# The last two feed-forward chunks of a layer stack, interleaved behind a shorter drain

## The chip, the cores and the metric

The kernel runs on one core of one Trainium2 chip. The metric is device time in microseconds (us) of one execution, start to end. Engines are called TensorE (PE, with PEld for its weight loads), VectorE (DVE), ScalarE (ACT), GpSimd (POOL) and SyncE (SP, which here only issues DMAs).

## The reference

The input is `x` of shape (2, 1024, 128), 2048 tokens of 128 features. Four stages follow: full causal attention (a), a stack of six layers (b), a gated linear scan (c), and the stack again. A stack takes the layer norm of its input, runs six layers on it and adds the result to its input. One layer is local attention and a feed-forward part, each with a residual:

```python
def attn_layer(x, Wqkv, qs, ksc, Wo): ...      # token shift first; 16 heads of 64, window 32
def ffn_layer(x, g, bln, W1, b1, W2, b2):      # on the token-shifted x
    mu = x.mean(-1, keepdims=True)
    var = ((x - mu) ** 2).mean(-1, keepdims=True)
    xn = (x - mu) / jnp.sqrt(var + 1e-05) * g + bln
    hg = xn @ W1 + b1
    a, gate = jnp.split(hg, 2, -1)             # 341 columns each
    return a * jax.nn.gelu(gate, approximate=False) @ W2 + b2
```

The token shift gives half of the features (64) the value of the token before.

## The kernel before

Activations lie transposed: 128 features on the partitions, 2048 tokens along the free dimension, in four chunks of 512 (`NC`, `CH`, `cs(k)`). `xT` is the residual of the whole network, `y` the running value inside a stack, `xs` the token-shifted copy of `y` that the projections read. All matrix products are fp32; one product of 128x512 is two MATMUL instructions in the trace. PSUM has eight banks of 128x512, `bank[0]` to `bank[7]`.

`stack(rep, ...)` is called twice. In it each engine has one program and semaphores order them; nothing is planned at run time. A layer is 32 slots (`PER`): the pairs of heads by chunks, 16 slots (`HALF`) for chunks 0 and 1 and 16 for chunks 2 and 3. `pipelined` writes out the slots: once for the first layer, a loop for the next five, and then `LAG` slots that drain what is still in flight. In slot `j`, `unit(k)` is the work that began `k` slots ago: projections at 0, scores at 2, the value product and output projection at 4, and VectorE's addition into `y` (L1112) at 5. So attention alone needs five draining slots.

The feed-forward part lags by `FLAG` = 19 slots and takes six slots per chunk (`ffn`, `FSTEPS`), one link of its chain in each: 0 mean (L982) and centring (L1115); 1 square (L1038), variance (L985), and ScalarE's Ln and Exp (L1017, L1035); 2 to 4 gain (L1144), bias (L1059), and one of `FT` = 3 pairs of W1 products each, `a` (L972) into bank 7 and `g` (L987) into bank 1, copied out with biases by VectorE (L1119) and ScalarE (L1021); 5 the GELU table load (L1069), the GELU (L1071) and GpSimd's product `hid*gel` (L828). Then W2's products (L976) and VectorE's addition (L1122). In the loop these links lie between attention work. After the last layer, two chunks remain when attention has ended: `LAG` = `HALF` + 1 = 17 draining slots, of which the slots from 3 on hold the twelve steps of chunk 2 and then chunk 3. There is one set of buffers (`fin`, `gel`, `hid`, `fsq`, `frs`), and each step waits for the step before it. SyncE shifts `y` into `xs` by two DMAs per chunk (L746). At the very end VectorE waits for all and adds `y` to `xT` in four instructions (L1164). The block ends there; stage c's first block follows the first stack, and the block with the output transposes (L206), ScalarE's copies (L214) and output DMAs (L222) follows the second.

Of the kernel before, what the change touches and what calls it, by code (L numbers as in the profile page):

```python
# [8 lines left out]
ALU = mybir.AluOpType  # L9
ACT = mybir.ActivationFunctionType  # L10
AX = mybir.AxisListType

P = 128
# [3 lines left out]
NC = N // CH  # L17
# [6 lines left out]
DEPTH, HEADS, DH, WIN = 6, 16, 64, 32  # L24
# [7 lines left out]
FT = -(-FI // P)  # L32
# [18 lines left out]
ONE = 1  # L51


def pipelined(eng, per, count, lag, slot, peel_last=False):


    def run(it, first=False, end=False):
        for j in range(lag if end else per):
            def unit(k, j=j):
                back, jj = divmod(j - k, per)  # L60
                if (first and back < 0) or (end and back >= 0):
                    return None
# [564 lines left out]
def stack(rep, ln_call, S, nc, w, c, bank, wide, xT, y, ident, identb, jmean, ln_eps, ss_eps, ss_back,  # L627
# [3 lines left out]
    with ExitStack() as st:  # L631
        def sb(name, shape, dt=F32):
            return st.enter_context(nc.sbuf_tensor(f"b{rep}_{name}", shape, dt))

        PAD = BLK
        xs = sb("xs", [P, N])
# [17 lines left out]
        prc = sb("prc", [P, 4, 2, CH])  # L654
# [11 lines left out]
        hid = sb("hid", [P, FT, CH])  # L666
        fin, gel = cen[:, 0, :], cen[:, 1:1 + FT, :]
        fsq, frs = sqr[:, 2, :], sqr[:, 3, :]

        L0 = DEPTH * rep  # L670
        FIRST = 1
        PER = 2 * 2 * PAIRS
        HALF = PER // 2
        FLAG = HALF + 3
        FSTEPS = 6
        LAG = HALF + 1
        ZERO = 8

        def um(u):
            return PER * (L0 + u[0]) + u[1], u[1] % 4  # L680
# [4 lines left out]
        def pair(u):  # L685
            return u[1] % HALF // 2

        def chunk(u):
            return 2 * (u[1] // HALF) + u[1] % 2

        def ffn(u):
            if u is None or u[1] % HALF >= 2 * FSTEPS:
                return None, None, None
            which, step = divmod(u[1] % HALF, FSTEPS)
            k = 2 * (u[1] // HALF) + which
            return step, k, NC * (L0 + u[0]) + k

        def ffn_out(u):
            if u is None or u[1] % HALF not in (FSTEPS, 2 * FSTEPS):
                return None, None  # L700
            k = 2 * (u[1] // HALF) + u[1] % HALF // FSTEPS - 1
            return k, NC * (L0 + u[0]) + k

        def closes(u):
            return pair(u) == PAIRS - 1
# [6 lines left out]
        with nc.Block() as block:  # L712
            @block.sync
            def _(sp):
# [23 lines left out]

                def slot(j, unit, sp=sp):
                    a, b, e = unit(0), unit(1), unit(5)  # L740
                    if e and closes(e):
                        C = NC * (L0 + e[0]) + chunk(e)
                        sp.wait_ge(S["y_add"], ONE + um(e)[0] + 1)
                        sp.wait_ge(S["fin_done"], ONE + 32 * C)
                        for to, frm in shifted(chunk(e)):
                            sp.dma_start(to, frm).then_inc(S["fin_done"], 16)  # L746
                    if b:
                        U, r = um(b)
                        sp.wait_ge(S["va_cp"], ONE + U + 1)
                        sp.wait_ge(S["vs_ld"], ONE + 32 * U)  # L750
                        sp.dma_start(vs[0:BLK, 4 * r:4 * r + 4, :], va[BLK:P, 4 * r:4 * r + 4, :]).then_inc(S["vs_ld"], 16)
                        sp.dma_start(vs[BLK:P, 4 * r:4 * r + 4, :], va[0:BLK, 4 * r + 1:4 * r + 5, :]).then_inc(S["vs_ld"], 16)
                        if b[1] > HALF and b[1] % 2 and not (isinstance(b[0], int) and b[0] == DEPTH - 1):
                            sp.wait_ge(S["va_mm"], ONE + U + 1)
                            sp.wait_ge(S["wqkv_ld"], ONE + 16 * (PAIRS * (L0 + b[0] + 1) + pair(b)))
                            load_qkv(b[0] + 1, pair(b))
                    if e:
                        U, r = um(e)
                        if e[1] > HALF and e[1] % 2 and not (isinstance(e[0], int) and e[0] == DEPTH - 1):
                            sp.wait_ge(S["wo_mm"], ONE + U + 1)  # L760
                            sp.wait_ge(S["wo_ld"], ONE + 16 * (PAIRS * (L0 + e[0] + 1) + pair(e)))
                            load_wo(e[0] + 1, pair(e))
                    if a and HALF <= j < HALF + 3:
                        li = a[0]
                        f = "L0_ffn_"
                        ffw = []
                        for i in range(2):
                            ffw.append((w1[:, i, 0:FI], w[f + "W1"][li, :, i * FI:(i + 1) * FI]))
                        for dst, nm in ((lng[:, 0:1], "ln_g"), (lng[:, 1:2], "ln_b"), (b2[:, 0:1], "b2")):
                            ffw.append((dst, w[f + nm][li, :].rearrange("(p a) -> p a", a=1)))  # L770
                        for h in range(2):
                            for i in range(FT):
                                n = P if i < FT - 1 else FR
                                ffw.append((b1[0:n, h, i:i + 1], w[f + "b1"][li, h * FI + i * P:h * FI + i * P + n]
                                            .rearrange("(p a) -> p a", a=1)))
                        ffw.append((w2[:, 0:FT - 1, :], w[f + "W2"][li, 0:(FT - 1) * P, :].rearrange("(i p) d -> p i d", p=P)))
                        ffw.append((w2[0:FR, FT - 1, :], w[f + "W2"][li, (FT - 1) * P:FI, :]))
                        if j == HALF and not (isinstance(li, int) and li == 0):
                            sp.wait_ge(S["y_done"], ONE + NC * (L0 + li))
                        for dst, src in ffw[5 * (j - HALF):5 * (j - HALF) + 5]:  # L780
                            sp.dma_start(dst, src).then_inc(S["ffw_ld"], 16)
                    if a:
                        U, r = um(a)
                        sp.wait_ge(S["pk_done"], ONE + U + 1)
                        if b:
# [12 lines left out]
                pipelined(sp, PER, DEPTH, LAG, slot, peel_last=True)  # L798

            @block.gpsimd  # L800
            def _(pool):
# [9 lines left out]
                def slot(j, unit, pool=pool):  # L811
# [13 lines left out]
                    if step == 5:  # L825
                        pool.wait_ge(S["f_acp"], ONE + FT * C + FT)
                        pool.wait_ge(S["f_gelu"], ONE + C + 1)
                        pool.tensor_tensor(hid[:, :, :], hid[:, :, :], gel, ALU.mult).then_inc(S["f_hid"], 1)  # L828
                pipelined(pool, PER, DEPTH, LAG, slot)

            @block.tensor
            def _(pe):
# [155 lines left out]

                pipelined(pe, PER, DEPTH, LAG, slot)

            @block.scalar
            def _(act):
                ln_act(act, ln_call)
# [2 lines left out]
                def slot(j, unit, act=act):  # L996
# [75 lines left out]
                pipelined(act, PER, DEPTH, LAG, slot)  # L1072

            @block.vector
            def _(dve):
# [22 lines left out]
                def slot(j, unit, dve=dve):  # L1098
# [845 lines left out]
```

## Time and profile before

| | us |
|---|---|
| median of 3 runs | 4513.82 (4508.88 to 4517.1) |
| the profiled execution | 4512.5 |
| its span, first to last instruction | 4510.8 |
| TensorE / VectorE / ScalarE / GpSimd busy | 4195.9 / 3451.3 / 3074.1 / 1811.6 |

The span leaves out 1.7 us of the profiled execution's time, which lie around it. Busy time is a mean over stages of different kinds and does not tell what bounds one of them. The mean granted TensorE clock is 0.959 of full speed.

### The profile page before, as it was taken

How to read it: one execution, taken by the hardware profiler on the slowest of the kernel's cores; microseconds unless marked ns; L12 is line 12 of the kernel's file. 1: busy time of each engine (PE TensorE's matmuls, PEld its weight loads, DVE VectorE, ACT ScalarE, POOL GpSimd, SP SyncE). 2: the span in 40 equal slices, each digit the busy share in tenths (PEclk: the TensorE clock that was granted, in tenths of full speed). 3: DMA queues.
4: the chain of work that ended last, by engine and by line, in shares of the span. 5: the costliest groups of instructions: out<-in, count | busy, mean ns of one | idle time of the engine just before them, and what ended most of it. 6: DMA issues, size and time to landing. Idle time of an engine off the chain costs nothing. (4 is left out here: it accounts for less than half of the span.)

```text
span 4510.8 us, 115928 instructions
## 1 busy us (share of the span) xinstructions
PE 4195.9 (93%) x44625; PEld 2511.7 (56%) x44625; DVE 3451.3 (77%) x4977; ACT 3074.1 (68%) x7028; POOL 1811.6 (40%) x1075
## 2 busy tenths in 40 slices
PE   7998999999999999999867589999999999999996
PEld 3443565655656655556436446555566556565663
DVE  5774888888888888888625478888888888888883
ACT  3555777777777777777652267777777777777774
POOL 3112444444444444444314434444444444444442
PEclk8997999999999999999976699999999999999998
DMA  2113444444443444444200044434444444444331
GB/s 42 30 21 83 99 100 99 103 103 93 105 104 88 106 99 103 99 92 98 61 10 3 3 122 108 101 85 110 101 96 101 97 102 101 94 104 105 89 92 36
DMA packets 239318, 382.06 MB, mean 85 GB/s; under 512 B 65636, under 2 KB 128736, under 8 KB 238472
## 3 DMA queue, kind: packets, MB, share of 16 engines
q1 hardware_dynamic: 238344, 373.28, 35.9%
q8 instruction: 386, 6.32, 0.6%
q10 hardware_dynamic: 384, 0.79, 0.1%
q14 instruction: 204, 1.67, 0.1%
HBM read 39.22 MB, written 1.05 MB: 9 GB/s over the span
## 5 line engine op out<-in xcount | busy, mean ns | idle before, releaser
L816 POOL TENSOR_TENSOR b_prob<-b_prob,b_rinv 128x768 f32<-128x768 f32 x384 | 565.1, 1472 | 1894.2 <-DVE b_rinv L1152 1894.2
L822 POOL TENSOR_TENSOR b_prc<-b_prc,b_sws 128x1024 f32<-128x1024 f32 x384 | 907.5, 2363 | 62.5 <-DMA b_sws<-b_prs 62.4
L1065 ACT ACTIVATE b_prob<-ps,b_nmx 128x96 f32<-128x96 f32 x3072 | 751.1, 363 | 0.0
L860 PEld LDWEIGHTS ps<-ident,b_prob 128*128 128x128 f32 x3072 | 378.1, 141 | 419.5 <-issue 297.4
L1093 DVE SCALAR_TENSOR_TENSOR b_prc<-ps,b_qks,b_rot 128x512 f32<-128x512 f32 x768 | 570.5, 743 | 12.8 <-ACT b_sq L1028 12.1
L1095 DVE SCALAR_TENSOR_TENSOR b_prs<-ps,b_qks,b_rot 128x512 f32<-128x512 f32 x768 | 569.3, 741 | 0.0
L1133 DVE TENSOR_TENSOR b_prc<-b_prc,ps 128x512 f32<-128x512 f32 x384 | 263.5, 686 | 387.2 <-PE ps L916 321.3
L1048 ACT ACTIVATE b_oT<-ps 128x512 f32<-128x512 f32 x384 | 227.2, 592 | 359.5 <-PE ps L874 359.5
L860 PE MATMUL ps<-ident,b_prob 128*128 128x128 f32 x3072 | 464.4, 274 | 4.4 <-ACT b_pT L1003 4.4
L1106 DVE SCALAR_TENSOR_TENSOR b_rsp<-b_rhi,b_minus_hi,b_rn 128x512 fp32r<-128x512 f32 x192 | 376.0, 1959 | 115.5 <-ACT b_rn L1014 115.5
L951 PE MATMUL ps<-b_wqkv,b_xs 128*128 128x128 f32 x3072 | 446.5, 289 | 1.4 <-DVE b_prs L1095 1.2
L1003 ACT ACTIVATE b_pT<-ps 128x512 f32<-128x512 f32 x724 | 436.3, 603 | 14.6 <-PE ps L860 11.1
L874 PE MATMUL ps<-b_pT,b_vs 128*64 128x64 f32 x6144 | 436.7, 234 | 0.3
L905 PE MATMUL ps<-b_xs,b_wqkv 128*128 128x512 f32 x768 | 405.6, 610 | 22.1 <-issue 14.6
L965 PE MATMUL ps<-b_oT,b_wo 128*128 128x512 f32 x768 | 412.3, 619 | 5.6 <-ACT b_oT L1048 5.6
L874 PE MATMUL ps<-b_pT,b_va 128*64 128x64 f32 x6144 | 399.6, 222 | 0.0
L921 PE MATMUL ps<-b_xs,b_wqkv 128*128 128x512 f32 x768 | 396.4, 597 | 0.5
L951 PEld LDWEIGHTS ps<-b_wqkv,b_xs 128*128 128x128 f32 x3072 | 373.3, 192 | 33.1 <-issue 7.3
L1157 DVE TENSOR_REDUCE b_nmx<-ps 128x8 f32<-128x768 f32 x384 | 353.3, 920 | 48.6 <-PE ps L940 48.1
L874 PEld LDWEIGHTS ps<-b_pT,b_vs 128*64 128x64 f32 x6144 | 307.7, 136 | 110.9 <-issue 64.5
L1149 DVE TENSOR_REDUCE b_ssm<-b_prob 128x8 f32<-128x768 f32 x384 | 361.5, 942 | 0.0
L1041 ACT ACTIVATE b_sq<-ps 128x512 f32<-128x512 f32 x384 | 229.4, 597 | 176.5 <-PE ps L921 174.9
(252 smaller groups left out, 7275.2 us busy)
## 6 DMA issues: line engine op xcount, KB each, us to landing
b_sws<-b_prs SPq DMA_DIRECT2D x1536, 128.0 KB, 2.3
b_vs<-b_va SPq DMA_DIRECT2D x768, 128.0 KB, 2.4
b_wqkv<-in_L_ffn_Wqkv SPq DMA_DIRECT2D x96, 192.0 KB, 2.8
b_xs<-y SPq DMA_DIRECT2D x132, 128.0 KB, 2.4
b_wo<-in_L_ffn_Wo SPq DMA_DIRECT2D x96, 64.0 KB, 2.2
b_xs<-y SPq DMA_DIRECT2D x44, 127.8 KB, 2.4
b_rot<-in_rot SPq DMA_DIRECT2D x2, 2048.0 KB, 7.8
b_w<-in_L_ffn_W SPq DMA_DIRECT2D x24, 170.5 KB
```

The source lines that it names most:

```text
L816: pool.tensor_tensor(prob[:, r, :, P - KEYS:P], prob[:, r, :, P - KEYS:P], rinv[:, r % 2, :].rearrange("p (b a) -> p b a", a=1).broadcast_ ...
L822: pool.tensor_tensor(prc[:, r, :, :], prc[:, r, :, :], sws[:, r % 2, :, :], ALU.add)\
L860: t = pe.transpose(bank[6][:, i * P:(i + 1) * P], prob[:, kd, 4 * e + 2 * h + m, :], ident[:, :])
L874: t = pe.matmul(bank[7][es, n * BLK:(n + 1) * BLK], v[:, es], pT[:, h, 2 * e + m, o * BLK:(o + 1) * BLK], start=(n == 0), stop=(n == NB - ...
L905: pe.matmul(bank[0][:, :], W[:, 0, :], X, start=True, stop=True).then_inc(S["q_mm"], 1)
L921: pe.matmul(bank[1][:, :], W[:, 1, :], X, start=True, stop=True).then_inc(S["k_mm"], 1)
L951: m = pe.matmul(bank[0][:, t * P:(t + 1) * P], xs[:, at:at + P], W[:, 2, :], start=(t == 0), stop=(t == 3), skip_group_check=True)
L965: pe.matmul(bank[3][:, :], wo[:, pair(d), :], oT[:, kd % 2, :], start=True, stop=True).then_inc(S["wo_mm"], 1)
L1003: act.activation(pT[:, h, :, :], bank[6].rearrange("p (i q) -> p i q", i=4), ACT.Copy)\
L1065: g = act.activation(prob[:, kb, i, P - KEYS:P], wide[0][:, e * CH + m * KEYS:e * CH + (m + 1) * KEYS], ACT.Exp, bias=nmx[:, kb % 2, i:i + 1])
L1093: dve.scalar_tensor_tensor(out=prc[:, r, i, :], in0=bank[i][:, :], scalar=scale, in1=rot[:, 2 * i, t], op0=ALU.mult, op1=ALU.mult)
L1095: dve.scalar_tensor_tensor(out=prs[:, r % 2, i, :], in0=bank[i][:, :], scalar=scale, in1=rot[:, 2 * i + 1, t], op0=ALU.mult, op1=ALU.mult) ...
```

## The change

The drain becomes five slots. The feed-forward parts of chunks 2 and 3 of the last layer leave the slots (`ending`) and are written out behind them, step by step for both chunks in turn. The second chunk has buffers of its own in tiles that attention no longer uses (`sqr`, `sq`, and `prc` as `more`), and the products have a bank each as far as eight reach. The shift of the two chunks goes from SyncE's DMAs to ScalarE copies, the product `hid*gel` from GpSimd to VectorE, and `y` is no longer summed first for these chunks: `add_x` adds it to `xT` early, and the last instruction adds W2's result to `xT` directly. Below, after the helpers, the new code of TensorE, then ScalarE's order, then VectorE's.

```diff
-        LAG = HALF + 1
+        LAG = 5
...
+        def ending(u):
+            return isinstance(u[0], int) and u[0] == DEPTH - 1 and u[1] >= HALF
...
-            if u is None or u[1] % HALF >= 2 * FSTEPS:
+            if u is None or ending(u) or u[1] % HALF >= 2 * FSTEPS:
...
+        end_fin, end_fsq, end_frs = (fin, sqr[:, 0, :]), (fsq, sqr[:, 1, :]), (frs, sq[:, 0, :])
+        end_gel, end_hid = (gel, sq[:, 1:1 + FT, :]), (hid[:, :, :], more[:, 0:FT, :])
+        end_mean, end_var, end_out = (0, 1), (2, 4), (0, 2)
+        end_g, end_a = ((5, 6, 0), (1, 5, 6)), ((7, 3, 2), (4, 7, 3))
...
-                    if e and closes(e):
+                    if e and closes(e) and not ending(e):
...
+                for n in range(2):
...
+                    pe.wait_ge(S["fin_done"], ONE + 32 * (CEND + n + 1))
+                    pe.matmul(bank[end_mean[n]], jmean[:, :], xs[:, cs(2 + n)], start=True, stop=True).then_inc(S["f_mean"], 1)
...
+                for n in range(2):
+                    pe.wait_ge(S["f_sq"], ONE + CEND + n + 1)
+                    pe.matmul(bank[end_var[n]], jmean[:, :], end_fsq[n], start=True, stop=True).then_inc(S["f_var"], 1)
...
+                for n in range(2):
+                    pe.wait_ge(S["f_in"], ONE + CEND + n + 1)
+                    for i in range(FT):
...
+                        elif n == 1:
+                            pe.wait_ge(S["f_gcp"], ONE + FT * CEND + i)
+                            pe.wait_ge(S["f_acp"], ONE + FT * CEND + i)
+                        pe.matmul(bank[end_g[n][i]], w1[:, 1, i * P:(i + 1) * P], end_fin[n], start=True, stop=True)\
+                            .then_inc(S["f_g"], 1)
+                        pe.matmul(bank[end_a[n][i]], w1[:, 0, i * P:(i + 1) * P], end_fin[n], start=True, stop=True)\
+                            .then_inc(S["f_a"], 1)
...
+                for n in range(2):
+                    pe.wait_ge(S["f_hid"], ONE + CEND + n + 1)
+                    for i in range(FT):
+                        m = pe.matmul(bank[end_out[n]], w2[:, i, :], end_hid[n][:, i, :], start=(i == 0), stop=(i == FT - 1))
+                    m.then_inc(S["f_out"], 1)
...
+                last_shift(0)
+                last_square(0)
+                last_shift(1)
+                last_rstd(0)
+                last_square(1)
+                last_in(0)
+                last_rstd(1)
+                last_in(1)
+                act.preload_act_table_set("gelu_and_others")
+                last_gate(0)
+                last_gelu(0)
+                last_gate(1)
+                last_gelu(1)
+                act.preload_act_table_set("natural_log_exp_and_others")
...
-                dve.wait_ge(S["y_done"], ONE + NC * (L0 + DEPTH))
-                for k in range(NC):
...
+                def last_product(n, dve=dve):
+                    dve.wait_ge(S["f_acp"], ONE + FT * (CEND + n) + FT)
+                    dve.wait_ge(S["f_gelu"], ONE + CEND + n + 1)
+                    dve.tensor_tensor(end_hid[n], end_hid[n], end_gel[n], ALU.mult).then_inc(S["f_hid"], 1)
...
+                add_x(0)
+                last_cen(0)
+                last_cen(1)
+                add_x(1)
+                last_norm(0)
+                last_norm(1)
+                for i in range(FT):
+                    last_hidden(0, i)
+                add_x(2)
+                add_x(3)
+                last_hidden(1, 0)
+                last_product(0)
+                last_hidden(1, 1)
+                last_hidden(1, 2)
+                last_out(0)
+                last_product(1)
+                last_out(1)
```

The helpers are what their names say: ScalarE's `last_shift` is two copies (`shifted(2 + n)`), of 64 partitions each, `last_square`, `last_rstd` (Ln, Exp), `last_in` (bias), `last_gate` (three copies with bias) and `last_gelu` (one instruction of 128x1536) do what L1038, L1017 with L1035, L1059, L1021 and L1071 did; `last_cen`, `last_norm` and `last_hidden` do what L1115, L1144 and L1119 did; `last_out` adds bank, bias `b2` and `xT` into `xT`.

## Rows read from the trace of the kernel before

**Rows 1.** Page, TensorE's granted clock in 40 slices of the span, tenths of full

```profile
PEclk8997999999999999999976699999999999999998
```

**Rows 2.** Windows from last y addition to block's end: us, busy by engine, clock, DMA

```profile
2233.75:2291.36 57.61, 27.51 (x43) 9.70 (x42) 11.29 (x16) 17.56 (x20) 6.83 (x2) 0.82 0.02 5
...
4443.71:4503.21 59.50, 29.41 (x43) 10.18 (x42) 11.29 (x17) 17.55 (x20) 6.83 (x2) 0.76 0.02 5
```

**Rows 3.** Timeline, SyncE's queue: start us, duration us, instruction

```profile
4438.77 6.07 SPq L746 DMA_DIRECT2D b_xs<-y  x4
```

**Rows 4.** Timeline, end of the second stack: start us, duration us, instruction, idle before it

```profile
4441.21 0.60 ACT L1048 ACTIVATE b_oT<-ps 128x512 f32<-128x512 f32 x1 [0.79 <-PE ps L874]
...
4443.02 0.69 DVE L1112 TENSOR_TENSOR y<-ps,y 128x512 f32<-128x512 f32 x1 [4.28 <-PE ps L965]
...
4444.60 0.63 ACT L1038 ACTIVATE sqr<-cen 128x512 f32<-128x512 f32 x1 [2.79 <-DVE cen L1115]
...
4445.37 1.10 PE L985 MATMUL ps<-sqr,jmean 128*128 128x512 f32 x2 [1.53 <-ACT sqr L1038]
4446.51 0.69 ACT L1017 ACTIVATE sqr<-ps,ln_eps 128x512 f32<-128x512 f32 x1 [1.28 <-PE ps L985]
...
4449.54 2.04 PE L972 MATMUL ps<-cen,b_w 128*128 128x512 f32 x2 [3.07 <-ACT cen L1059]
```

**Rows 5.** Groups by line in 4443.7 to 4503.3: busy us, mean ns, idle us before

```profile
L976 PE MATMUL ps<-b_hid,b_w 128*128 128x512 f32 x12 | 9.4, 948 | 14.5 <-POOL b_hid L828 14.5
...
L828 POOL TENSOR_TENSOR b_hid<-b_hid,cen 128x1536 f32<-128x1536 f32 x2 | 6.8, 3417 | 51.8 <-ACT cen L1071 51.8
L1119 DVE TENSOR_SCALAR b_hid<-ps,b_b 128x512 f32<-128x512 f32 x6 | 4.5, 750 | 17.1 <-PE ps L972 17.1
L1021 ACT ACTIVATE cen<-ps,b_b 128x512 f32<-128x512 f32 x6 | 4.1, 688 | 17.6 <-PE ps L987 17.6
...
L1071 ACT ACTIVATE cen<-cen 128x1536 f32<-128x1536 f32 x2 | 3.0, 1482 | 0.0
L1069 ACT ACT_TABLE_LOAD x2 | 2.6, 1283 | 0.0
...
L1164 DVE TENSOR_TENSOR xT<-xT,y 128x512 f32<-128x512 f32 x4 | 2.5, 686 | 0.0
...
L1144 DVE SCALAR_TENSOR_TENSOR cen<-cen,b_lng,sqr 128x512 f32<-128x512 f32 x2 | 1.5, 752 | 6.0 <-ACT sqr L1035 6.0
L1122 DVE SCALAR_TENSOR_TENSOR y<-ps,b_b,y 128x512 f32<-128x512 f32 x2 | 1.5, 748 | 12.0 <-PE ps L976 12.0
L1059 ACT ACTIVATE cen<-cen,b_lng 128x512 f32<-128x512 f32 x2 | 1.4, 721 | 1.6 <-DVE cen L1144 1.6
L1115 DVE TENSOR_TENSOR cen<-b_xs,ps 128x512 f32<-128x512 f32 x2 | 1.4, 687 | 13.1 <-PE ps L982 13.1
L1017 ACT ACTIVATE sqr<-ps,ln_eps 128x512 f32<-128x512 f32 x2 | 1.4, 687 | 2.6 <-PE ps L985 2.6
```

**Rows 6.** Timeline, the six W2 instructions of an earlier chunk, inside the loop

```profile
4416.46 2.74 PE L976 MATMUL ps<-b_hid,b_w 128*128 128x512 f32 x6
```

**Rows 7.** Windows of TensorE alone: us, busy, clock, DMA share, GB/s

```profile
2239.50:2242.70 3.20, 3.12 (x4) 0.50 0.00 0
4448.00:4458.00 10.00, 7.53 (x8) 0.50 0.00 0
4503.50:4507.20 3.70, 3.65 (x16) 0.50 0.26 72
```

**Rows 8.** Groups by line, VectorE, whole span: a product of 128x1536

```profile
L1755 DVE TENSOR_TENSOR c_bl<-ps,c_lmask 128x1536 f32<-128x1536 f32 x8 | 14.0, 1747 | 0.0
```

**Rows 9.** Timeline, the last block: the output transposes and the copies

```profile
4503.54 3.65 PE L206 MATMUL ps<-ident,xT 128*128 128x128 f32 x16 [3.65 <-PEq L712]
4504.66 0.60 ACT L214 ACTIVATE otok<-ps 128x512 f32<-128x512 f32 x1 [11.86 <-PE ps L206]
...
4507.22 0.60 ACT L214 ACTIVATE otok<-ps 128x512 f32<-128x512 f32 x1 [0.26 <-PE ps L206]
```

More of the change, by code:

```diff
@@ L698, in ffn_out @@
         def ffn_out(u):
-            if u is None or u[1] % HALF not in (FSTEPS, 2 * FSTEPS):
+            if u is None or ending(u) or u[1] % HALF not in (FSTEPS, 2 * FSTEPS):
                 return None, None
@@ L702, in ffn_out @@
             return k, NC * (L0 + u[0]) + k
+        UALL, CEND = PER * (L0 + DEPTH), NC * (L0 + DEPTH - 1) + 2
+        more = prc[:, :, :, :].rearrange("p a b c -> p (a b) c")
+        end_fin, end_fsq, end_frs = (fin, sqr[:, 0, :]), (fsq, sqr[:, 1, :]), (frs, sq[:, 0, :])
+        end_gel, end_hid = (gel, sq[:, 1:1 + FT, :]), (hid[:, :, :], more[:, 0:FT, :])
+        end_mean, end_var, end_out = (0, 1), (2, 4), (0, 2)
+        end_g, end_a = ((5, 6, 0), (1, 5, 6)), ((7, 3, 2), (4, 7, 3))
         def closes(u):
@@ L989, in _ @@
                 pipelined(pe, PER, DEPTH, LAG, slot)
+                pe.wait_ge(S["va_cp"], ONE + UALL)
+                for n in range(2):
+                    if n == 1:
+                        pe.wait_ge(S["pk_done"], ONE + UALL)
+                        pe.wait_ge(S["f_gcp"], ONE + FT * CEND)
+                    pe.wait_ge(S["fin_done"], ONE + 32 * (CEND + n + 1))
+                    pe.matmul(bank[end_mean[n]], jmean[:, :], xs[:, cs(2 + n)], start=True, stop=True).then_inc(S["f_mean"], 1)
@@ new lines, in _ @@
+                pe.wait_ge(S["qn_done"], ONE + UALL)
+                pe.wait_ge(S["exp_done"], ONE + UALL)
+                for n in range(2):
+                    pe.wait_ge(S["f_sq"], ONE + CEND + n + 1)
+                    pe.matmul(bank[end_var[n]], jmean[:, :], end_fsq[n], start=True, stop=True).then_inc(S["f_var"], 1)
+                pe.wait_ge(S["pt_cp"], ONE + 2 * UALL)
+                pe.wait_ge(S["o_cp"], ONE + UALL)
+                pe.wait_ge(S["y_done"], ONE + CEND)
+                pe.wait_ge(S["y_add"], ONE + UALL)
@@ new lines, in _ @@
+                for n in range(2):
+                    pe.wait_ge(S["f_in"], ONE + CEND + n + 1)
+                    for i in range(FT):
+                        if n == 0 and i == 2:
+                            pe.wait_ge(S["f_cen"], ONE + CEND + 1)
+                            pe.wait_ge(S["f_lnv"], ONE + CEND + 1)
+                        elif n == 1 and i == 0:
+                            pe.wait_ge(S["f_cen"], ONE + CEND + 2)
+                            pe.wait_ge(S["f_lnv"], ONE + CEND + 2)
+                        elif n == 1:
[5 more added lines that the diff above has]
+                            .then_inc(S["f_a"], 1)
@@ L991, in _ @@
+                pe.wait_ge(S["f_gcp"], ONE + FT * CEND + FT)
+                pe.wait_ge(S["f_acp"], ONE + FT * CEND + FT)
+                for n in range(2):
[3 more added lines that the diff above has]
+                    m.then_inc(S["f_out"], 1)
             @block.scalar
@@ L1072, in _, with last_shift, last_square, last_rstd @@
                 pipelined(act, PER, DEPTH, LAG, slot)
+                def last_shift(n, act=act):
+                    act.wait_ge(S["y_add"], ONE + UALL - 1 + n)
+                    act.wait_ge(S["va_mm"], ONE + UALL)
+                    for to, frm in shifted(2 + n):
+                        act.activation(to, frm, ACT.Copy).then_inc(S["fin_done"], 16)
+                def last_square(n, act=act):
+                    act.wait_ge(S["f_cen"], ONE + CEND + n + 1)
+                    act.activation(end_fsq[n], end_fin[n], ACT.Square).then_inc(S["f_sq"], 1)
+                def last_rstd(n, act=act):
+                    act.wait_ge(S["f_var"], ONE + CEND + n + 1)
+                    act.activation(end_frs[n], bank[end_var[n]], ACT.Ln, bias=ln_eps[:, 0:1]).then_inc(S["f_lnv"], 1)
+                    act.wait_ge(S["f_lnv"], ONE + CEND + n + 1)
+                    act.activation(end_frs[n], end_frs[n], ACT.Exp, scale=-0.5).then_inc(S["f_rstd"], 1)
+                def last_in(n, act=act):
+                    act.wait_ge(S["f_norm"], ONE + CEND + n + 1)
+                    act.activation(end_fin[n], end_fin[n], ACT.Identity, bias=lng[:, 1:2]).then_inc(S["f_in"], 1)
+                def last_gate(n, act=act):
+                    for i in range(FT):
+                        act.wait_ge(S["f_g"], ONE + FT * (CEND + n) + i + 1)
+                        act.activation(end_gel[n][:, i, :], bank[end_g[n][i]], ACT.Identity, bias=b1[:, 1, i:i + 1])\
+                            .then_inc(S["f_gcp"], 1)
+                def last_gelu(n, act=act):
+                    act.wait_ge(S["f_gcp"], ONE + FT * (CEND + n) + FT)
+                    act.activation(end_gel[n], end_gel[n], ACT.Gelu).then_inc(S["f_gelu"], 1)
+                last_shift(0)
[12 more added lines that the diff above has]
+                act.preload_act_table_set("natural_log_exp_and_others")
             @block.vector
@@ L1161, in _, with add_x @@
                 pipelined(dve, PER, DEPTH, LAG, slot)
-                dve.wait_ge(S["y_done"], ONE + NC * (L0 + DEPTH))
-                for k in range(NC):
-                    dve.tensor_tensor(xT[:, cs(k)], xT[:, cs(k)], y[:, cs(k)], ALU.add).then_inc(S["x_done"], 1)
+                def add_x(k, dve=dve):
+                    if k < 2:
+                        dve.wait_ge(S["y_done"], ONE + CEND - 1 + k)
+                    else:
+                        dve.wait_ge(S["y_add"], ONE + UALL - 3 + k)
+                    dve.tensor_tensor(xT[:, cs(k)], xT[:, cs(k)], y[:, cs(k)], ALU.add).then_inc(S["x_done"], 1)
@@ new lines, in last_cen, with last_norm @@
+                def last_cen(n, dve=dve):
+                    dve.wait_ge(S["f_mean"], ONE + CEND + n + 1)
+                    dve.tensor_tensor(end_fin[n], xs[:, cs(2 + n)], bank[end_mean[n]], ALU.subtract).then_inc(S["f_cen"], 1)
+                def last_norm(n, dve=dve):
+                    dve.wait_ge(S["f_rstd"], ONE + CEND + n + 1)
+                    dve.scalar_tensor_tensor(out=end_fin[n], in0=end_fin[n], scalar=lng[:, 0:1], in1=end_frs[n],
+                                             op0=ALU.mult, op1=ALU.mult).then_inc(S["f_norm"], 1)
@@ new lines, in last_hidden @@
+                def last_hidden(n, i, dve=dve):
+                    dve.wait_ge(S["f_a"], ONE + FT * (CEND + n) + i + 1)
+                    dve.tensor_scalar(end_hid[n][:, i, :], bank[end_a[n][i]], b1[:, 0, i:i + 1], None, ALU.add).then_inc(S["f_acp"], 1)
+                def last_product(n, dve=dve):
+                    dve.wait_ge(S["f_acp"], ONE + FT * (CEND + n) + FT)
+                    dve.wait_ge(S["f_gelu"], ONE + CEND + n + 1)
+                    dve.tensor_tensor(end_hid[n], end_hid[n], end_gel[n], ALU.mult).then_inc(S["f_hid"], 1)
@@ new lines, in last_out @@
+                def last_out(n, dve=dve):
+                    dve.wait_ge(S["f_out"], ONE + CEND + n + 1)
+                    dve.wait_ge(S["x_done"], ONE + NC * rep + 3 + n)
+                    x = xT[:, cs(2 + n)]
+                    dve.scalar_tensor_tensor(out=x, in0=bank[end_out[n]], scalar=b2[:, 0:1], in1=x, op0=ALU.add, op1=ALU.add)\
+                        .then_inc(S["y_done"], 1)
+                add_x(0)
+                last_cen(0)
+                last_cen(1)
+                add_x(1)
@@ L1167, in stage_c @@
+                last_norm(0)
+                last_norm(1)
+                for i in range(FT):
+                    last_hidden(0, i)
[8 more added lines that the diff above has]
+                last_out(1)
 def stage_c(nc, w, c, sem, ps, bank, xT, y, ident, jmean, ln_eps, cen, sqr, rstd, ln_pe, ln_act, ln_dve, norm_done, cs, ln_call):
```

## The prediction

> **What bounds the kernel now.** I read the page first. TensorE's granted clock is full in all slices of the span but a few: at the start, at the middle (the first stack's end and stage c) and at the very end [rows 1]. The loops of the stacks are TensorE's; the change leaves every slot of them as it is. What it touches comes once per stack, so I cut two windows with one rule: from the end of the last addition into `y` (L1112, the last work of attention) to the end of the block. They last 57.61 us in the first stack and 59.50 us in the second, TensorE is busy for 27.5 and 29.4 of them, VectorE for 11.3, ScalarE for 17.6, and nothing is moved by DMA to speak of [rows 2]. So no engine bounds them: a chain of dependent steps does. The table by line says whose turns these are: GpSimd waits 51.8 us for two products, the W2 products wait 14.5 us for GpSimd, ScalarE's three copies per chunk 17.6 us for TensorE, VectorE's 17.1 us [rows 5]. The next blocks start only when all engines are through, so each microsecond off these windows is one off the kernel.
>
> **The change part by part.** Let 0 be the end of the last L1112, 4443.71 in the second stack (4443.02 + 0.69) [rows 4]. The new tail can be laid out on that scale; what is before 0 stays.
>
> Durations, by row: ScalarE from SBUF 0.63 [rows 4], from PSUM 0.69, with the bias of L1059 0.72, GELU of 1536 columns 1.48, table load 1.28; VectorE 0.69 for centring, 0.75 for L1144, L1119 and L1122, 0.69 for an `xT` addition (0.63 from one to the next in a row of four) [rows 5]. One product is two MATMULs; three of them in a row took 2.74 at full clock inside the loop [rows 6], which is 0.86 each and 0.17 until the last result is out; at half clock 1.71 each. A result passes to ScalarE or VectorE in 0.04 (L985 ends at 4446.47, L1017 starts at 4446.51) [rows 4]; to TensorE in 0.14 (L1038 ends at 4445.23, L985 starts at 4445.37) [rows 4].
>
> Layer norms, at full clock. ScalarE is free from its last `b_oT` copy at 4441.81 [rows 4], which is -1.9. SyncE's four DMAs, 6.07 us with their wait [rows 3], go; chunk 2's had landed before TensorE was free, so here ScalarE's copies (two of 64 partitions each, a form that no row shows; I price each at the 0.63 of 128 partitions, and between half of that and twice that the tail moves by -0.6 to +1.3 for each chunk) put the mean at -0.4, where TensorE is nearly free anyway. Result at 0.64, VectorE after `add_x(0)` centres until 1.37, the square is done at 2.04. Now the order written for ScalarE tells: chunk 3's shift stands behind this square, 2.07 to 3.36, though its data were there at 0. TensorE in turn has chunk 3's mean ahead of chunk 2's variance: 3.50, then the variance's result at 5.39. Ln and Exp to 6.79, gain to 7.58, the bias behind square(1) to 8.34. Chunk 3's variance is at TensorE 7.59 to 8.45, so the W1 products start at 8.48. In the chain before, this stretch took 4449.54 - 4443.71 = 5.8 for one chunk and again, behind the W2 products, for the other.
>
> W1 products: twelve in a row, 12 x 0.86 = 10.3, to 18.8. Beside them ScalarE does Ln, Exp and bias of chunk 3 (to 11.57), the table load (12.88), three copies (15.04) and the GELU (16.55); VectorE copies chunk 2's three `a` results, adds `y` to `xT` twice, and multiplies `hid*gel` until 18.34. This product is new on VectorE: GpSimd's took 3.42 [rows 5]; VectorE's only fp32 product of 128x1536 in the trace took 1.75, one input in PSUM [rows 8]. I take 1.75, the same size on the same engine; bounds are ScalarE's 1.48 for as many columns and GpSimd's 3.42, which would add 1.7 at each of two places. Hand-over of banks does not stop the twelve: the second chunk's later pairs wait for copies that end at 13.6 and 14.3, before TensorE comes to them at 15.4 and 17.1. That is the gain of separate banks: before, every pair waited for the copy of the pair before.
>
> Out: W2 products of chunk 2 from 18.8 with the result at 21.55, VectorE's addition to 22.34. Here again an order costs: chunk 3's product stands behind that addition on VectorE, 22.34 to 24.09, though its GELU was done at 20.35. W2 products 24.23 to 26.98, addition to 27.77. The four final additions (2.5 from first to last) are inside.
>
> So at full clock the new tail is 27.8 us, against 57.6 and 59.5.
>
> **TensorE's clock.** Before, both first W1 stretches ran at half clock: 3.2 us of it shown in the first stack, 10 us in the second [rows 7], after a layer norm in which TensorE stood idle 3.07 us [rows 4]. The new layer norms hold gaps too: 2.9 us between the two means, 2.2 before the second variance. I expect the clock to fall in them and to come back in the dense W1 stretch, as in the first stack. Price: chunk 3's mean and chunk 2's variance 0.86 each, chunk 3's variance and the start of the W1 stretch together 1.7: 3.4, so 31.2 us per tail. If the clock stays full: 27.8. If it is half all along, the second stack's case at its worst: 22 products on TensorE's path (4 means and variances, 12 of W1, 6 of W2), 0.86 each, make 18.9 more, 46.7. The nearest rows are the two stacks before; the denser W1 stretch (twelve products without a wait, where there were two at a time) decides for the lower part. The gap ahead of the last W2 products is 2.7 us, shorter than the 3.07 above, and follows a dense stretch; I count them full.
>
> The clock page of the Trainium skill (TensorE: Matmul & The Clock Gate, Part 1) says that the clock is halved after an idle spell of TensorE and restored by a busy one. The trace agrees on the whole, but the fall before L972 came after a layer norm with products in it [rows 4, 7], so gaps with little work between them are enough here. By that rule of the Trainium skill alone the new layer norms, never idle for long, would keep the clock: that is the first rival below.
>
> The Trainium skill also budgets about 2.7 us for a switch of ScalarE's table (ScalarE: Activation LUTs, Rules for kernel authors). The rows have 1.28 [rows 5]. By that figure of the Trainium skill the first copies would end 1.4 later and so would chunk 2's product, which TensorE waits for: 1.4 per tail more at most. The row decides.
>
> **Next blocks.** The output transposes start after 3.6 us of idle TensorE and ran at half clock, 3.65 us; the fourth copy starts 3.68 behind the first transpose [rows 7, 9]. After the new tail TensorE is idle for about 1.1 us. At full clock the first copy can start 0.5 earlier, and then copies of 0.60 follow each other without waiting, 1.86 from the first to the fourth where it was 2.56: 1.2 us earlier in all. Stage c's first layer norm opens the same way; I put 1.0 there (0 to 2). Together 2.2, 0 if the clock is half.
>
> **Sum.** Second stack 59.5 - 31.2 = 28.3, first 57.6 - 31.2 = 26.4, next blocks 2.2: 56.9 less. On the profiled execution's own 4512.5 us that is 4455.6; on the median of the runs, 1.3 above it, 4456.9, which I round to 4457.
>
> **The rivals.** First, the clock stays full in both tails: for it speaks that no gap is longer than 2.9, against it the fall before. Time: 31.7 + 29.8, and 3 in the next blocks: 64.5 less, 4449. Chance 0.17.
>
> Second, the clock stays half through both tails: the second stack before shows 10 us in one piece while TensorE was busy for 7.5 of them [rows 7]. 12.8 + 10.9 = 23.7 less, 4490. Against it: the W1 stretch is now busy without pause. Chance 0.04.
>
> Third, the interleaving is worth less than it looks: queues in order (VectorE and ScalarE serve both chunks) leave the second chunk waiting in more places than I found, as a wait for a bank that comes on top. If both tails end at 39 instead of 31: 20.5 + 18.6, and 2 in the next blocks, 41 less, 4473. For it speaks that three such places are already in my layout; against it, that they are counted. Chance 0.11.
>
> Fourth, slower than before. The tail itself cannot do it: even at half clock it is shorter. It would have to be the loops, whose code is the same but lies in a program of another length; if instructions came later there, each of some 384 slots would pay. It decides from 57/384 = 0.15 us per slot; at 0.2 us the time would be 4457 + 77 = 4534. Nothing in the rows shows such a stall, and the full clock in the loops [rows 1] speaks against starved engines. Chance 0.02.
>
> My forecast has 0.66. A measurement of this kernel tells 0.2% (9 us) from no change. The forecast and the first three rivals are all faster by more, 0.98 together, of which I move 0.01 to no change for what I have not foreseen; slower keeps 0.02. The range takes the first rival and 3 us for the spread of runs below, 4446, and reaches to near the third above, 4470.
>
> **What would show it.** Windows of 28 to 34 us from the last L1112 to the block's end in both stacks. Twelve W1 products with no gap between them; ScalarE's shift of chunk 3 starting about 2 us after its `y` was ready; the `hid*gel` product on VectorE at 1.75; the clock below full in the layer norms and full at the W2 products; transposes in about 2 us. The loops' slots as long as before. The prediction is wrong if the W1 stretch is broken by waits, if the partial ScalarE copies cost much more than 0.63, if the clock falls again between the two W2 stretches, or if any time moves outside these windows.

## The result, and the profile after

The changed kernel takes 4448.52 us (median of 4 runs, 4442.27 to 4466.87), the kernel before 4513.18 (4 runs). The ratio is 0.986, with a 95% interval of 0.9839 to 0.988: faster, by 64.7 us of medians. The profiled execution took 4450.76, 61.7 less than the one before; its span is 4449.0.

I cut the span at events that both kernels have: the end of the last addition into `y` (L1112, now L1207) in each stack, the end of the last VectorE instruction of the tail, the end of stage c's last addition. Us by stage:

| | first part with stack 1 | tail 1 | stage c | stack 2 | tail 2 | output |
|---|---|---|---|---|---|---|
| before | 2233.75 | 57.61 | 302.31 | 1850.04 | 59.50 | 7.59 |
| after | 2236.03 | 32.03 | 294.24 | 1849.99 | 29.59 | 7.12 |

The windows of the changed kernel (us, then busy time with instructions in brackets for PE, PEld, DVE, ACT, POOL, then clock, DMA share, GB/s), against [rows 2]:

```profile
2236.03:2268.06 32.03, 24.07 (x44) 9.44 (x42) 14.37 (x18) 15.81 (x20) 0.00 (x0) 0.84 0.00 0
2268.06:2562.30 294.24, 185.66 (x5333) 149.27 (x5333) 140.29 (x260) 110.41 (x177) 115.01 (x168) 0.69 0.02 6
4412.29:4441.88 29.59, 21.63 (x44) 8.42 (x42) 14.37 (x19) 15.70 (x20) 0.00 (x0) 0.88 0.00 0
4441.88:4449.00 7.12, 1.94 (x16) 1.73 (x16) 0.00 (x1) 2.07 (x4) 0.00 (x0) 0.87 0.56 150
```

A tail is the stretch in the second column, from the last addition into `y` to the block's end. TensorE is now busy for 24.1 and 21.6 us of the two tails, three quarters of them; before it was less than half. The clock is 0.84 and 0.88, not full. Stage c, which was not touched, lost 8 us too; I come back to it.

The timeline of the second tail (start us, duration us, instruction, idle before it), against [rows 4]:

```profile
4410.28 1.27 ACT L1128 ACTIVATE b_xs<-y 64x512 f32<-64x512 f32 x2
...
4411.60 0.69 DVE L1207 TENSOR_TENSOR y<-ps,y 128x512 f32<-128x512 f32 x1 [4.28 <-PE ps L975]
...
4413.55 0.63 ACT L1132 ACTIVATE sqr<-cen 128x512 f32<-128x512 f32 x1 [2.00 <-DVE cen L1267]
4414.08 1.26 ACT L1128 ACTIVATE b_xs<-y 64x512 f32<-64x512 f32 x2
...
4415.49 1.16 PE L1007 MATMUL ps<-b_xs,jmean 128*128 128x512 f32 x2 [2.70 <-ACT b_xs L1128]
...
4416.44 1.92 PE L1012 MATMUL ps<-sqr,jmean 128*128 128x512 f32 x2
...
4422.18 1.54 PE L1029 MATMUL ps<-cen,b_w 128*128 128x512 f32 x2
...
4427.85 1.02 PE L1029 MATMUL ps<-sqr,b_w 128*128 128x512 f32 x2
...
4430.59 1.75 DVE L1281 TENSOR_TENSOR b_hid<-b_hid,cen 128x1536 f32<-128x1536 f32 x1
...
4433.00 2.74 PE L1038 MATMUL ps<-b_hid,b_w 128*128 128x512 f32 x6
...
4433.06 1.48 ACT L1152 ACTIVATE b_sq<-b_sq 128x1536 f32<-128x1536 f32 x1
...
4435.78 0.75 DVE L1287 SCALAR_TENSOR_TENSOR xT<-ps,b_b,xT 128x512 f32<-128x512 f32 x1 [1.82 <-PE ps L1038]
4436.45 1.75 DVE L1281 TENSOR_TENSOR b_prc<-b_prc,b_sq 128x1536 f32<-128x1536 f32 x1
...
4438.25 2.84 PE L1038 MATMUL ps<-b_prc,b_w 128*128 128x512 f32 x6 [2.51 <-DVE b_prc L1281]
...
4441.13 0.75 DVE L1287 SCALAR_TENSOR_TENSOR xT<-ps,b_b,xT 128x512 f32<-128x512 f32 x1 [2.94 <-PE ps L1038]
...
4442.21 1.94 PE L206 MATMUL ps<-ident,xT 128*128 128x128 f32 x16 [1.12 <-PEq L722]
```

0 is 4412.29 here. Chunk 3's shift (the two ScalarE copies at 4414.08) starts 1.79 after its `y` was ready, behind chunk 2's square. Its mean and the variance behind it fill 4415.49 to 4418.36. The W1 products start at 9.89 and run without a gap from chunk 2 into chunk 3 to the W2 products at 20.71. Chunk 3's GELU ends at 4434.54 and its product starts 1.91 later, behind chunk 2's last addition. The transposes follow at 1.94 us for all sixteen, where they took 3.65 [rows 9].

TensorE's clock in it (us, busy time, clock, DMA share, GB/s), against [rows 7]:

```profile
4415.50:4422.10 6.60, 4.64 (x6) 0.57 0.00 0
4423.60:4441.80 18.20, 14.98 (x35) 1.00 0.00 0
2262.90:2267.20 4.30, 4.29 (x6) 0.64 0.00 0
```

It was half for most of the stretch from the second mean into the first W1 product, full from there to the end in tail 2; in tail 1 it was half again at the start of the last W2 products, after a pause of 2.51 us, and they took 4.36 us instead of 2.84:

```profile
2262.91 4.36 PE L1038 MATMUL ps<-b_prc,b_w 128*128 128x512 f32 x6 [2.51 <-DVE b_prc L1281]
```

### The profile page after: what moved, and what is told of

Read it like the earlier page. It is cut to its first block and busy times, and to the rows that moved or that the text cites. A ratio compares the mean times of both kernels' runs of the same rounds, so it can differ in the third digit from the quotient of the medians.

```text
span 4449.0 us, 115926 instructions
## 1 busy us (share of the span) xinstructions
PE 4171.8 (94%) x44625; PEld 2499.4 (56%) x44625; DVE 3462.9 (78%) x4981; ACT 3073.0 (69%) x7032; POOL 1796.9 (40%) x1071
## 5 line engine op out<-in xcount | busy, mean ns | idle before, releaser
L1115 ACT ACTIVATE b_prob<-ps,b_nmx 128x96 f32<-128x96 f32 x3072 | 751.1, 363 | 0.0
L915 PE MATMUL ps<-b_xs,b_wqkv 128*128 128x512 f32 x768 | 405.6, 610 | 23.8 <-issue 15.4
L931 PE MATMUL ps<-b_xs,b_wqkv 128*128 128x512 f32 x768 | 395.9, 597 | 0.5
```

The source lines that it names most:

```text
L915: pe.matmul(bank[0][:, :], W[:, 0, :], X, start=True, stop=True).then_inc(S["q_mm"], 1)
L931: pe.matmul(bank[1][:, :], W[:, 1, :], X, start=True, stop=True).then_inc(S["k_mm"], 1)
L1115: g = act.activation(prob[:, kb, i, P - KEYS:P], wide[0][:, e * CH + m * KEYS:e * CH + (m + 1) * KEYS], ACT.Exp, bias=nmx[:, kb % 2, i:i + 1])
```

## The experiments

Each starts from the changed kernel, unless it says otherwise. Tails are in the order first, second. The swaps, the filled kernel and the changed kernel beside them were executed four times each, both together six times; the others once. The same kernel's stages differ from run to run, by the clock above all: the changed tails measured 29.6 to 32.0 us, so a single tail tells nothing below 2 us.

**One chunk after the other.** The banks, buffers, VectorE's product, the early additions and ScalarE's shift stay; only the order of each engine is serial:

```diff
-                last_shift(0)
-                last_square(0)
-                last_shift(1)
...
+                last_shift(0)
+                for n in range(2):
+                    last_square(n)
+                    last_rstd(n)
+                    last_in(n)
+                    act.preload_act_table_set("gelu_and_others")
+                    last_gate(n)
+                    last_gelu(n)
+                    act.preload_act_table_set("natural_log_exp_and_others")
+                    if n == 0:
+                        last_shift(1)
```

and likewise on TensorE and VectorE.

> The two chunks one after the other, all else as in the changed kernel (banks, VectorE's product, early additions to xT, ScalarE's shift). My theory: most of the gain is the interleaving. Each chunk's chain alone is about 19 us at full clock (6 for the layer norm, 5.3 for the six W1 products, 4 until the product hid*gel is made, 3 for W2), and half clock after each pause adds 2 to 3, so the tails are 41 to 46 us, 12 to 15 longer than interleaved. Rival: the gain is in the cheaper links (GpSimd's product to VectorE, additions moved, a bank for each product): then the tails stay below 36 us. No change to the kernel: near 58.

Measured: tails 44.89 and 44.96 us, 4482.21 us in all. Its first tail in the view by windows:

```profile
2229.31:2274.20 44.89, 27.97 (x44) 10.08 (x42) 14.65 (x18) 18.81 (x22) 0.00 (x0) 0.81 0.00 0
```

So the gain per tail has two halves: 12.7 and 14.5 us come from the cheaper links, 13 to 15 from the interleaving. "Most of it is the interleaving" was too much; "below 36" was wrong. Of the first half, by rows of before, 3.3 are two products at 1.75 instead of 3.42 [rows 5, 8] and 2.5 the four additions [rows 5]. Two more terms stand in the traces. ScalarE's table load, which stood between the last copy and the GELU before, is hidden under the W1 products here: 1.28 for each chunk, 2.6 in all. The first line is before, the second the serial order:

```profile
4461.36 1.28 ACT L1069 ACT_TABLE_LOAD   x1
...
4434.32 1.28 ACT L1148 ACT_TABLE_LOAD   x1
```

And from the first W1 product to the end of the last copy the second tail took 11.8 and 9.6 us for the two chunks before, 6.9 and 7.0 in the serial order: 7.6 less, for a bank to each product and for the clock, which no run separates. The four make 16.0 of the 14.5 measured in this tail; the serial order gives 1.5 back elsewhere.

**The product back on GpSimd.**

```diff
-                last_product(0)
...
-                last_product(1)
...
+                for n in range(2):                       # after GpSimd's slots
+                    pool.wait_ge(S["f_acp"], ONE + FT * (CEND + n) + FT)
+                    pool.wait_ge(S["f_gelu"], ONE + CEND + n + 1)
+                    pool.tensor_tensor(end_hid[n], end_hid[n], end_gel[n], ALU.mult).then_inc(S["f_hid"], 1)
```

> The two products hid*gel of the tail back on GpSimd. GpSimd takes 3.42 us, VectorE 1.75. My theory: GpSimd begins when the GELU is done and is not behind VectorE's other work, so the first W2 stretch starts about 0.6 us later and the second at the same time or 0.1 earlier: tails within 1 us of the changed kernel's 32.0 and 29.6. Rival: the faster product is a full term of the gain, 1.7 at each of two places, tails 3.3 us longer.

Tails 29.51 and 30.78, 4456.86 us in all: no loss against the four tails of the changed kernel (29.6 to 32.0). In this order the faster product buys nothing, since TensorE is busy with W1 during the first, and the second stood in VectorE's queue: in the second tail, from chunk 3's GELU to its W2 products it is 3.71 us with VectorE's 1.91 of waiting and 1.75 of work, and 3.62 with GpSimd's 3.42. So the prediction's bound for this term, 1.7 more at each of two places with GpSimd's time, was too wide: its layout has room for the second (GELU done at 20.35, the product on VectorE at 24.09), and the first held TensorE for 0.3 us only. Whether the product counts in the serial order or after the swaps below, no run shows.

**The shift back on SyncE's DMAs**, ScalarE's `last_shift` left out:

```diff
+                for n in range(2):                       # after SyncE's slots
+                    sp.wait_ge(S["y_add"], ONE + UALL - 1 + n)
+                    for to, frm in shifted(2 + n):
+                        sp.dma_start(to, frm).then_inc(S["fin_done"], 16)
```

> The shift of the last two chunks back to SyncE's DMAs, ScalarE's four copies left out. Chunk 3's copies end 3.05 us after the last y addition in the changed kernel; two DMA issues and some 2.4 us until they land end at about 2.9 to 3.1. My theory: tails equal within 0.6 us. Rival: ScalarE's copies are a gain of their own against the DMAs: tails 1 to 2 us longer.

Tails 30.66 and 30.70, 4450.84 us: equal within the spread. Chunk 3's mean, which waits for the shift, started 3.04 us after the last `y` addition with the DMAs and 3.20 with the copies. A copy of 64 partitions took ScalarE 0.62; moving the shift there bought nothing.

**Two swaps of order.**

```diff
-                last_square(0)
                 last_shift(1)
+                last_square(0)
...
-                last_out(0)
                 last_product(1)
+                last_out(0)
```

> Two swaps of order, nothing else: ScalarE shifts chunk 3 before it squares chunk 2, and VectorE makes chunk 3's product hid*gel before it adds chunk 2's W2 result. My theory, by the changed kernel's trace: chunk 3's shift can end at 1.3 instead of 3.05 after the last y addition, and its mean and chunk 2's variance behind it come 1.75 earlier; chunk 3's product can start at 22.3 instead of 24.2, so the last W2 stretch starts 1.8 earlier. Tails 3.6 us shorter, near 26 and 28. Rival: these waits are not what ends last and the clock eats what they give (the clock falls anyway): under 1 us.

4438.45 us (4435.72 to 4439.05, 4 runs); the changed kernel, timed beside it on the same chip, 4448.95 (4446.12 to 4452.07, 4 runs). Ratio to before 0.9825 (0.9806 to 0.9845). Tails 24.00 and 25.70, 6.7 and 3.9 less than the changed kernel's second profile. The timeline of its second tail, where 0 is 4404.49:

```profile
4404.58 1.28 ACT L1128 ACTIVATE b_xs<-y 64x512 f32<-64x512 f32 x2 [0.83 <-issue]
...
4423.10 2.74 PE L1038 MATMUL ps<-b_hid,b_w 128*128 128x512 f32 x6
...
4424.75 1.76 DVE L1281 TENSOR_TENSOR b_prc<-b_prc,b_sq 128x1536 f32<-128x1536 f32 x1 [0.70 <-ACT b_sq L1152]
...
4426.56 0.30 PEld L1038 LDWEIGHTS ps<-b_prc,b_w 128*128 128x128 f32 x2 [1.55 <-DVE b_prc L1281]
```

The shift starts at 0.1; chunk 3's product waits for its GELU alone and is under way while W2 of chunk 2 runs, so TensorE stands 0.72 us between the two W2 stretches instead of 2.51. Both tails gained more than the 3.6 expected. In the first the clock was 1.00 throughout, and 24.0 is 3.5 under the 27.5 that the changed order takes at full clock (next experiment): the other 3.3 there are the clock. In the second, with the same pauses, the first W1 products ran at half clock and the mean was 0.93, so closing these pauses does not keep the clock every time. This is the best version that I ran.

**Filled pauses.** Eight products whose results nobody reads, put into TensorE's three pauses:

```diff
+                def idle(m):
+                    for _ in range(m):
+                        pe.matmul(bank[6], jmean[:, :], xs[:, cs(0)], start=True, stop=True)
```

three after the first mean, two before the second variance, three before the last W2 stretch (after a wait for all `f_gcp`).

> The changed kernel, with products whose results nobody reads in TensorE's pauses of the tail (three between the two means, two ahead of the second variance, three ahead of the last W2 stretch), to keep the clock up. My theory: half clock costs the changed tails 1.9 and 4.2 us over the layout at full clock; filled, both tails are 27 to 28.5 us, the granted clock 1.00 in them. Rival: the clock falls all the same, or the filling delays what waits behind it: 29.5 to 32 as before or more.

Tails 27.47 and 27.48 us, clock 1.00:

```profile
4423.58:4451.06 27.48, 26.32 (x60) 1.00 0.00 1
```

That is the layout at full clock, 27.8, within 0.3 (W1 from 8.2, W2 from 18.6, the last W2 from 23.8, where the layout has 8.5, 18.8 and 24.2), and so the clock's share of the changed kernel's tails is 2.1 to 4.6 us. But the kernel got slower: 4464.97 us (4459.91 to 4470.96, 4 runs) against 4448.95. All of it is in stack 2, 1872.84 us. Its layers 2 to 5 took 311.5, 310.8, 312.0 and 308.4 where they have 305 to 307 in the changed kernel; stack 1 is unchanged. The waits of TensorE's matmuls over the loop of stack 2 (us in total, times, longest), filled kernel:

```profile
PE ps L915 <- issue: 15.1, 4, 4.1
```

and changed kernel:

```profile
PE ps L915 <- issue: 3.5, 4, 1.2
```

This wait comes once per turn, at the first instruction of the loop's body. TensorE's timeline at one turn of the filled kernel:

```profile
3776.89 1.45 PE L986 MATMUL ps<-b_hid,b_w 128*128 128x512 f32 x3
3782.45 2.07 PE L915 MATMUL ps<-b_xs,b_wqkv 128*128 128x512 f32 x2 [4.11 <-issue]
...
3786.03 1.91 PE L931 MATMUL ps<-b_xs,b_wqkv 128*128 128x512 f32 x2
```

It stood 4.1 us with all inputs there, and the clock had fallen when it came back: the products L915 and L931 take 2.07 and 1.91 instead of 1.1 and 1.0.

**Both together.**

> Both: the two swaps and the filled pauses. If the two act on different terms, they add up: tails of 24 to 25 us at full clock, some 11 us less than the changed kernel over the two tails, 4439 where it has 4450. If they pay for the same pause, 26 to 27.

4466.15 us (4454.7 to 4471.65, 6 runs); tails 26.91 and 26.92. They do not add up: with the pauses closed by the swaps, the filling stands in the way of what it waited for. In the second tail chunk 3's product was ready at 4453.52, but its W2 products started at 4455.26, behind the filling. The tails are 1.2 and 2.9 us longer than with the swaps alone. Stack 2 is slow again, 1873.16.

**What makes stack 2's loop slow.** Filling in one tail only (`if rep == 0`, `if rep == 1`), then in the first tail with products of 8 columns instead of 512, then only three of these. They were executed once each, on another chip, where the kernel before took 4526.14 us, so their totals are not compared with the others; the stages and turns are:

> The changed kernel with the eight unread products in the first stack's tail alone. In the kernel filled in both, the layers 2 to 5 of the second stack took 311 us instead of 306: TensorE stood 3.8 us at each turn of its loop, where it is 0.9. My theory: what is put ahead of that loop in TensorE's program does it, so with the filling in the first tail alone the second stack is again near 1874 us, its turns 12 to 13 us from y addition to y addition instead of 8. Rival: the filling of the second tail, or the full clock at the end, is what matters: 1850 to 1858.

> The changed kernel with the eight unread products in the second stack's tail alone. Theory: nothing is put ahead of either loop, both stacks as in the changed kernel (1850 to 1858 us for the second), the second tail 27.5, the first 30.5 to 32. Rival: second stack near 1874.

> As the filling in the first tail alone, at the same places and in the same number, but each product 8 columns wide instead of 512: the same instructions, next to no time. If the number of instructions ahead of the loop decides, the second stack is near 1874 us. If what the products do to TensorE (clock, heat, time) decides, it is 1850 to 1858. [...]

> As before, but three short products instead of eight. If any instructions ahead of the loop do it: near 1874 us. If it is a matter of where the loop comes to lie: anything between 1850 and 1874, and the turns of the loop show which.

| | stack 2, us | a turn, y addition to y addition, us | total |
|---|---|---|---|
| changed kernel | 1849.99, 1850.45 | 7.7 to 8.5 | 4450.76, 4446.12 |
| eight in the first tail | 1868.34 | 10.7 to 12.7 | 4470.48 |
| eight in the second tail | 1853.40 | 7.7 to 8.4 | 4450.19 |
| eight short ones in the first | 1874.42 | 10.3 to 14.4 | 4468.97 |
| three short ones in the first | 1858.75 | 8.9 to 9.5 | 4456.03 |

The waits in the kernel with the eight short ones, and below them those in the kernel with three:

```profile
PE ps L915 <- issue: 16.2, 4, 4.5
...
PE ps L926 <- issue: 4.6, 4, 1.4
PE ps L915 <- issue: 3.2, 4, 1.0
```

So neither the work of the filling does it nor the clock (in the first tail 1.00 with the eight long ones, 0.88 with the eight short ones), but instructions ahead of the loop in TensorE's program. Three cost 1.2 us a turn, eight 2 to 6. With three the wait at L915 is what it was, and the new one stands at L926, a little further on in the body: the number of instructions ahead decides also where in the loop TensorE waits. That it is the fetch of the loop's code from another place I only infer; no view shows it. The turns carry this reading, not the totals of stack 2: in the nine runs with nothing put ahead of its loop, stack 2 took 1850.0 to 1856.1.

**The two kernels once more.**

> The kernel before once more, for the spread of the stages that the change does not touch. In the two profiles stage c took 302.3 us before and 294.2 after. If that is the clock's spread from run to run, this run's stage c can lie anywhere between 290 and 306 and the tails repeat near 58 and 59 (within 3 us, by the clock). If the change makes stage c shorter, this run shows 302 within 1 us.

> The changed kernel once more, timed and with a second profile. Tails near 30 and 32 us by the clock, stage c between 294 and 301 if its length is the clock's spread, 294 within 1 us if it is fixed by the change. Time 4442 to 4467, median near 4450.

Before again: tails 57.85 and 58.54, stage c 301.78, stack 1 2228.56, stack 2 1854.86, 4510.9 us. Changed again: tails 30.73 and 29.60, stage c 296.98, stack 1 2229.51, stack 2 1850.45.

## Why the prediction was right

**What bounds the tail.** Right: a chain of dependent links, one off for one off. The two tails gave 25.6 and 29.9 us, 55.5 of the 61.7 between the profiled executions; forecast 54.7.

**The layout.** Right term by term. Shift behind square at 2.07 (measured 1.79), W1 to W2 12 x 0.86 (18.8 - 8.5 = 10.3; measured 10.8, its first product partly at half clock), the `hid*gel` product 1.75 (1.75), chunk 3's product behind chunk 2's addition (from 24.16 in place of 22.3, the W1 stretch having started 1.4 late and taken 0.5 more). The filled kernel measured the sum at full clock: 27.5 for 27.8. The two places that I named as orders that cost were the two that the swaps took out.

**The clock.** The mechanism was right, the size rough. I had it fall in the layer norms and come back in the W1 stretch, 3.4 us; the four tails show 2.1, 2.1, 3.3 and 4.6. One part of the step was wrong: the last W2 stretch was at half clock in one tail, after a pause of 2.51 us, where I counted it full; this happened in the first tail of both profiles of the changed kernel, and a clock falling between the two W2 stretches was one of the prediction's own signs of being wrong. The first rival, the rule of the Trainium skill (TensorE: Matmul & The Clock Gate, Part 1) taken at its word, that the clock is kept unless TensorE is idle for a spell, did not come true: the clock fell at about 4416, though TensorE had made a mean until 4412.8 and was at the next from 4415.5, 2.70 us idle between them. Its time, 4449, was met all the same, for another reason (below, what I left out). The second rival did not occur.

**ScalarE's table.** The load was 1.28 again, and the three copies and the GELU followed as laid out. The budget of 2.7 us of the Trainium skill (ScalarE: Activation LUTs, Rules for kernel authors) is not seen.

**Next blocks.** The term of 2.2 was mis-sized in its parts. Stage c's first layer norm ends 2.0 earlier (its first result, L143, starts 5.5 instead of 7.5 us after the tail), not 1.0. The first line is before, where the tail ended at 2291.36, the others after, where it ended at 2268.06:

```profile
2298.88 0.68 DVE L143 TENSOR_TENSOR y<-cen,rstd 128x512 f32<-128x512 f32 x1
...
2267.31 0.75 DVE L1287 SCALAR_TENSOR_TENSOR xT<-ps,b_b,xT 128x512 f32<-128x512 f32 x1 [4.45 <-PE ps L1038]
...
2273.55 0.69 DVE L143 TENSOR_TENSOR y<-cen,rstd 128x512 f32<-128x512 f32 x1
```

And the output takes 0.5 less, not 1.2, though the copies end 1.5 earlier. The trace shows where the rest went: SyncE's four DMA issues took 0.41 to 0.84 us each, where they took 0.37 to 0.41 before, and the median from issue to landing was 2.8 instead of 2.5.

**What I left out.** Stage c as a whole: 302.3 and 301.8 in the two profiles of the kernel before, 294.2 to 300.8 in the twelve that have the changed tail in some form, 297.1 on average. Beyond the 2.0 it is between nothing and 6 us less, and all twelve lie below both. Its clock is 0.66 before and 0.69 after, with the same 5333 instructions of TensorE busy for 195.1 us before and 185.7 after:

```profile
2291.36:2593.67 302.31, 195.11 (x5333) 156.57 (x5333) 137.66 (x260) 110.38 (x177) 114.67 (x168) 0.66 0.02 6
```

The amount changes from run to run with the same kernel (294.2 and 297.0), so a part is the clock's spread; whether the change moved the rest, and by what, stays open. A time that moves outside the tails was another of the prediction's signs of being wrong. Of the 8.4 us between 4456.9 and 4448.5, 4.8 are in the profiled executions: 7.1 more than the 1.0 forecast came off stage c, 0.8 more off the tails, and the output (0.7) and the first part (2.3) took some back. The other 3.6 are where the profiled execution stood among its runs, 1.3 below the median in the forecast and 2.2 above it after. All this lies within a spread of 25 us between the best and the worst of four runs, so that the total came so close is in part luck; the tails are the part that the prediction explains.

**The third rival** (queues leave the second chunk waiting, 39 us per tail) did not occur; its known places are in the sum. **The fourth**, slower loops through code at another place, did not occur here: layers 2 to 5 take 305 to 307 us in both kernels. But I had argued it away by the full clock in the loops, and that was no argument: the wait is there in the kernel before (L905, 0.7 us on average at each turn of the second loop), and eight more instructions ahead of the loop made it about 4.

## What to carry to other kernels

When a pipeline's drain is a chain of dependent links on one item after another, write the last items out side by side with buffers of their own: here about half of the gain came from that and half from cheaper links. Then lay out each engine's queue in order and look for an instruction that waits while the one behind it is ready: two swaps that such a layout named gave 10 us more, 7 of them on paper and the rest by the clock. A diagnostic that adds instructions ahead of a loop has to be read stage by stage, since the loop may pay for it.

## What the runs showed of the hardware

Eight instructions of next to no work in TensorE's program ahead of a loop of 32 slots made each turn of the loop 2 to 6 us longer, three made it about 1.2 longer, and eight behind the loop (here of 512 columns) did nothing. ScalarE's copy of 64 partitions by 512 columns took 0.62 us, as much as one of 128 partitions (0.63). VectorE's product of 128x1536 in fp32, all in SBUF, took 1.75 us, as with one input in PSUM; GpSimd's took 3.42 to 3.77.
